# Filter scores of a batch taken in one place, by row halves into two PSUM banks

## The chip, the cores and the metric

The kernel runs on one core of a Trainium2 chip. The metric is the device time of one execution in microseconds, as the median of several runs; less is better. A core has a matrix engine (TensorE: PE in the rows, its weight loads PEld), a vector engine (VectorE: DVE), an activation engine (ScalarE: ACT), a general engine (GpSimd: POOL) and a queue for transfers (SyncE: SP). Matrix results land in PSUM, here eight banks of 512 floats for each of 128 partitions; the other engines take them from there.

## The reference, cut to what matters

A layer normalisation, an attention and a mixture of experts with product keys, all added to the input. The case has 16 batches of 256 tokens and a width of 128. The change lies in the mixture, in the step that is called the filter here: the scores `s0`, `s1` and their best four.

```python
x = L0_attn_x                                   # [16, 256, 128]
xn = layernorm(x)
x = x + attention(xn) + experts(xn)             # attention: 16 heads of 8
# experts
q = (xn @ Wq + bq).reshape(B, S, 8, 32)         # 8 heads of 32 features
q = batchnorm(q)
q0, q1 = l2norm(q[..., :16]), l2norm(q[..., 16:])
s0 = einsum('bshq,kq->bshk', q0, l2norm(sub_key0))    # 32 scores for each head and side
s1 = einsum('bshq,kq->bshk', q1, l2norm(sub_key1))
ts0, ti0 = top_k(s0, 4); ts1, ti1 = top_k(s1, 4)
w = softmax(all 16 sums of a pair); idx = 32 * ti0 + ti1
out = sum over pairs of up[idx] * gelu(down[idx] . xn) * w
```

## The kernel before

The program has one instruction stream for each engine, written by hand, and the engines meet by counting semaphores. After the inputs are projected (up to about 56 us) comes one long loop of 128 slots, eight to each of the 16 batches, one for each pair of attention heads. I call the slot's number modulo eight k. Every stream walks the same slots, and what it does in a slot, and in what order, is fixed by the code.

In every slot PE takes the second scores of one pair (`sj`, L651: K times Q into the PSUM tensor `SJ`), the first scores of a later pair (`si`, L615, into `SI`), and in every second slot the attention's values (`values`, L675: sixteen matmul instructions into the bank `psO`). DVE reduces each `si` to its maxima (L1002), ACT takes the exponential of each `sj` (L449). `SJ` has one copy, so `sj` of the next slot waits for the exponential of this one. `psO` holds two halves, one for each eight heads: `values` fills a half in two slots (k=2 and 4, or k=6 and the next 0), and ACT copies it out a slot later (L419, into `Osb`, semaphore `o_ev`; in k=1 the half that k=0 completed).

Between these lie the filter's steps of an earlier batch. Nearly all of their PSUM results go through one bank, `psM`, one after the other:

- k=0: POOL has split the row maxima (L1276, L1278, semaphore `ms`), PE transposes them into `psM` (`turn_maxima`, L695), ACT copies them out (L463), and two small DMAs on SP carry them to where `sj` of k=3 reads them (`max_rows`, L283).
- k=1: PE takes the scores of the batch's first 128 tokens into `psM` (`scores`, L705; the lines L709 are its matmuls): two matmuls, each of 128 feature rows by 256 columns, the keys `kblk` being block diagonal. In float32 a matmul is two matmul instructions.
- k=2: ACT copies them to `s_sb` (L410), DVE takes the best eight of each group of 32 (L1028, 16 instructions). After `values` and `si` PE takes the scores of the second 128 tokens (L796 waits until ACT's copy has freed `psM`).
- k=3: ACT copies them, DVE takes their best eight; PE waits for that copy (L804) before it transposes the products of another batch into `psM` (`turn_products`, L713; L716).
- k=3 and 4: ACT takes the best four (`best_four`, L377). k=4 to 7: DVE marks them with sixteen match-and-replace steps (L1052), and POOL works out ranks and weights. In k=5 ACT copies a transposed output (L456), DVE inverts its denominators (L1060, `rden`), and POOL, which waits for that, normalises (L1218, `on`). After it come POOL's rank steps, and behind these in the same queue the split of the maxima for the next k=0.

The scores of batch 0 come while other work is under way, those of batch 15 after the loop, in two banks of `SI` (L815). The token tiles and heads of a batch are numbered 0 to 15 in `s_sb`: eight heads of the first tile, then eight of the second.

Of the kernel before, what the change touches and what calls it, by code (L numbers as in the profile page):

```python
# [24 lines left out]
ACT = mybir.ActivationFunctionType  # L25
AX = mybir.AxisListType.X

P = 128
# [18 lines left out]
def program(nc, x, Wq, bq, Wl, bl, Wk, bk, Wv, bv, Wo, bo,  # L47
            fWq, fbq, gamma, beta, key0, key1, down, up, const, scratch, out):
    B, S, D = x.shape
# [5 lines left out]
    BT = S // P  # L55
# [6 lines left out]
    FH, FQ = 8, 32  # L62
# [20 lines left out]
    with ctx:  # L83
# [85 lines left out]
        psG = [SJ[:, 0:512], SJ[:, 512:1024]]  # L169
        psS = [SI[0][:, 0:512], SI[0][:, 512:1024]]  # L170
# [3 lines left out]
        REPLACED = (0, 4, 10, 12, 16)  # L174

# [134 lines left out]
        def _(act):  # L310
# [66 lines left out]
            def best_four(b, t):  # L377
                hs = slice(FH * t, FH * (t + 1))
                act.wait_ge(s["t8"], 2 * b + t + 1)
                if b >= 1:  # L380
                    act.wait_ge(s["mr"], 4 * b)
                A(top4[:, hs, 0:TOP], top8[:, hs, 1, 0:TOP], ACT.Copy).then_inc(s["t4"], 1)

            for slot in range(NSLOT):
# [17 lines left out]
                if k in (2, 3) and 0 <= b < B:  # L402

                    t = k - 2
                    act.wait_ge(s["fs"], 2 * b + t + 1)
                    act.wait_ge(s["pad"], 1)
                    if b >= 1:
                        act.wait_ge(s["mr"], 4 * b)
                        act.wait_ge(s["sel"], b)
                    A(s_sb[:, FH * t:FH * (t + 1), :, 0:NK].rearrange("p h a k -> p (h a) k"),  # L410
                      psM.rearrange("p (g k) -> p g k", k=NK), ACT.Copy).then_inc(s["fs_ev"], 1)
# [68 lines left out]
            def last_scores(t):  # L480
                act.wait_ge(s["fs"], 2 * LB + t + 1)
                A(s_last[:, FH * t:FH * (t + 1), :, 0:NK].rearrange("p h a k -> p (h a) k"),
                  psS[t].rearrange("p (g k) -> p g k", k=NK), ACT.Copy).then_inc(s["fs_ev"], 1)
# [47 lines left out]
        def _(pe):  # L531
# [173 lines left out]
            def scores(b, t, dst):  # L705

                tok = (BT * b + t) * P
                for r in range(2):
                    last = mm(dst[:, 256 * r:256 * (r + 1)], fqT[:, r, tok:tok + P],  # L709
                              kblk[:, :, :].rearrange("p g k -> p (g k)"), start=True, stop=True)  # L710
                last.then_inc(s["fs"], 1)
# [39 lines left out]
            for slot in range(NSLOT):  # L751
# [14 lines left out]
                if m >= 0 and m % 2 == 0:  # L766
                    values(m // 2)
                if slot < NPAIR * B - 1:

                    si(slot + 1)  # L770
                if FILTER <= slot < FILTER + NC:
                    norms(slot - FILTER)
# [15 lines left out]
                if k in (1, 2) and 0 <= b < B:  # L788

                    if b == 0 and k == 1:  # L790
                        pe.wait_ge(s["kblk"], 1)
                    if k == 1:
                        pe.wait_ge(s["mt_ev"], b + 1)
                        pe.wait_ge(s["ff"], b + 1)
                    else:
                        pe.wait_ge(s["fs_ev"], 2 * b + 1)  # L796
                    scores(b, k - 1, psM)
# [17 lines left out]
            for t in range(BT):  # L815
                scores(LB, t, psS[t])
# [47 lines left out]
        def _(dve):  # L864
# [128 lines left out]
            for slot in range(NSLOT):  # L993
# [25 lines left out]
                if k in (2, 3) and 0 <= b < B:  # L1019

                    t = k - 2
                    dve.wait_ge(s["fs_ev"], 2 * b + t + 1)
                    if b >= 1:
                        dve.wait_ge(s["sel"], b)
                        dve.wait_ge(s["t4"], 2 * b)
                    for h in range(FH * t, FH * (t + 1)):
                        for a in range(2):
                            last = V.max(top8[:, h, a, :], s_sb[:, h, a, 0:NK])  # L1028
                    last.then_inc(s["t8"], 1)
# [10 lines left out]
                if k in (4, 5, 6, 7) and 0 <= b < B:  # L1040

                    quarter = k - 4
                    t = quarter // 2
                    dve.wait_ge(s["t4"], 2 * b + t + 1)
                    if b >= 1:
                        dve.wait_ge(s["pr"], 4 * b - 2 * (1 - t))
                    for h in range(REPLACED[quarter], REPLACED[quarter + 1]):
                        if quarter == 1 and h == FH:
                            dve.wait_ge(s["t4"], 2 * b + 2)
                            if b >= 1:  # L1050
                                dve.wait_ge(s["pr"], 4 * b)
                        last = V.match_replace(r_sb[:, h, :], top4[:, h, :], s_sb[:, h, 1, :], NEG)  # L1052
                    last.then_inc(s["mr"], 1)
# [38 lines left out]
            for t in range(2):  # L1092
                dve.wait_ge(s["fs_ev"], 2 * LB + t + 1)
                for h in range(FH * t, FH * (t + 1)):
                    for a in range(2):
                        last = V.max(top8[:, h, a, :], s_last[:, h, a, 0:NK])
                last.then_inc(s["t8"], 1)
            for t in range(2):
                dve.wait_ge(s["t4"], 2 * LB + t + 1)
# [53 lines left out]
        def _(pool):  # L1153
# [166 lines left out]
            for t in range(2):  # L1320
# [11 lines left out]
                pool.wait_ge(s["t8"], 2 * b + t + 1)  # L1332
                pool.wait_ge(s["mr"], 4 * b)
                V.tensor_copy(top4[:, hs, 0:TOP], top8[:, hs, 1, 0:TOP]).then_inc(s["t4"], 1)
# [60 lines left out]
```

## Time and profile before

| | |
|---|---|
| median of 3 runs | 353.02 us (352.87 to 353.14) |
| the profiled execution | 350.41 us |
| its span, first to last instruction | 348.3 us |
| busy: PE, DVE, ACT, POOL | 311.8, 320.7, 265.2, 274.0 us |
| mean granted TensorE clock | 0.99 of full speed |
| largest groups | DVE L1002 153.2 us, ACT L449 119.2 us, PE L690 68.7 us |

The page of the profile has a chain of work that ended last, which it follows back from the last instruction: 63% of it is PE, 17% ACT and 9% DVE. All rows are from that one execution. In the rows of the timeline a line gives the start from the beginning of the span, the time from the first start to the last end of the instructions merged in it, engine and line, the operation, the tensors out<-in, the shapes out<-in, how many (x), and in brackets how long the engine stood idle before it and what ended that. An instruction on DVE or ACT can start a little before the one ahead of it has ended, so two neighbours can overlap by some hundredths.

### The profile page before, as it was taken

What the parts mean: (1) busy time and instruction counts of PE and PEld (TensorE: products, weight loads), DVE (VectorE), ACT (ScalarE), POOL (GpSimd) and SP (SyncE); (2) the same over time, 40 slices, a digit from 0 to 9 for tenths busy, and PEclk for the clock granted to TensorE, in tenths of its full rate; (3) what the DMA queues carried; (4) which work ended last, traced back from release to release, by engine and by line L of the source; (5) the groups of instructions that cost most, each with busy time, mean ns of one, the idle gap of its engine ahead of it and who ended that gap; (6) DMA issues with size and microseconds to landing.
All of it is one profiled execution on the core that took longest, in us unless ns stands there. A gap on an engine that the chain in (4) does not pass through costs nothing.

```text
span 348.3 us, 9625 instructions
## 1 busy us (share of the span) xinstructions
PE 311.8 (90%) x3024; PEld 168.1 (48%) x3024; DVE 320.7 (92%) x1393; ACT 265.2 (76%) x446; POOL 274.0 (79%) x527
## 2 busy tenths in 40 slices
PE   3898997976999999999999989999999999998886
PEld 2455554332445554545454545454544545555445
DVE  6599989989999999999999999999999999999681
ACT  3699995978687877787768686868677787878781
POOL 6288885835869898989898989888898989898930
PEclk9999999996999999999999999999999999999999
DMA  4765666217121112213030303030303030000001
GB/s 122 212 172 138 175 179 179 75 53 128 37 63 48 47 51 60 78 34 93 18 91 22 108 3 109 2 108 5 108 19 92 19 92 20 3 20 1 19 17 30
DMA packets 45886, 24.81 MB, mean 71 GB/s; under 512 B 5452, under 2 KB 45708, under 8 KB 45836
## 3 DMA queue, kind: packets, MB, share of 16 engines
q1 hardware_dynamic: 45836, 24.20, 25.9%
q8 instruction: 24, 0.39, 0.5%
q14 instruction: 26, 0.21, 0.2%
HBM read 15.54 MB, written 8.39 MB: 69 GB/s over the span
## 4 chain that ended last, share of the span: by engine, by line
PE 63%; ACT 17%; DVE 9%; issue 8%; POOL 1%; ACTq 0%; POOLq 0%; DVEq 0%
PE bank L690 13%; PE SJ L670 9%; PE bank L716 9%; PE bank L709 9%; PE SI L629 6%; ACT Eb L449 5%; PE bank L744 3%; ACT s_sb L410 3%; PE SJ L779 2%; ACT onT L432 2%; PE bank L745 2%; ACT fwq_in L456 2%; PE bank L736 2%; PE bank L646 1%; ACT fqT L328 1%
## 5 line engine op out<-in xcount | busy, mean ns | idle before, releaser
L1002 DVE TENSOR_REDUCE negm<-SI 128x4 f32<-128x1024 f32 x128 | 153.2, 1208 | 1.0 <-PE SI L629 1.0
L449 ACT ACTIVATE Eb<-SJ 128x1024 f32<-128x1024 f32 x117 | 119.2, 1019 | 10.3 <-PE SJ L670 10.2
L690 PE MATMUL bank<-Eb,vhat 128*18 128x256 f32 x1024 | 68.7, 386 | 0.9 <-ACT Osb L488 0.9
L670 PE MATMUL SJ<-QS,KS 50*128 50x256 bf16 x484 | 48.2, 278 | 10.3 <-ACT Eb L449 9.8
L1305 POOL TENSOR_TENSOR prod<-r_sb,a 128x1024 f32<-128x1024 f32 x28 | 53.5, 1910 | 0.0
L629 PE MATMUL SI<-KS,QS 48*128 48x256 bf16 x512 | 50.6, 277 | 1.8 <-DVE negm L1002 1.8
L1028 DVE MAX8 top<-s_sb 128x8 f32<-128x32 f32 x480 | 47.6, 177 | 2.9 <-ACT s_sb L410 0.8
L1052 DVE MATCH_REPLACE8 r_sb<-top,s_sb 128x36 f32<-128x36 f32 x240 | 40.5, 181 | 0.0
L690 PEld LDWEIGHTS bank<-Eb,vhat 128*18 128x18 f32 x1024 | 24.2, 98 | 26.8 <-issue 13.7
L629 PEld LDWEIGHTS SI<-KS,QS 48*128 48x128 bf16 x512 | 18.7, 95 | 35.2 <-issue 21.1
L716 PE MATMUL bank<-cst,prod 128*128 128x128 f32 x240 | 32.4, 278 | 3.3 <-ACT s_sb L410 3.3
L709 PE MATMUL bank<-kblk,fqT 128*128 128x256 f32 x120 | 33.9, 405 | 0.4 <-ACT s_sb L410 0.4
L410 ACT ACTIVATE s_sb<-bank 128x512 f32<-128x512 f32 x30 | 17.9, 596 | 20.2 <-PE bank L709 19.3
L670 PEld LDWEIGHTS SJ<-QS,KS 50*128 50x128 bf16 x484 | 14.0, 95 | 38.8 <-ACT Eb L449 27.1
L716 PEld LDWEIGHTS bank<-cst,prod 128*128 128x128 f32 x240 | 25.7, 141 | 10.4 <-issue 9.9
L1175 POOL TENSOR_TENSOR Eb<-Eb,parts 128x512 f32<-128x512 f32 x16 | 18.2, 1156 | 15.7 <-ACT parts L318 11.8
L709 PEld LDWEIGHTS bank<-kblk,fqT 128*128 128x128 f32 x120 | 20.3, 189 | 8.3 <-issue 3.1
L1052 DVE MATCH_VALUE_LOAD r_sb<-top,s_sb 128x8 f32 x240 | 19.1, 80 | 0.0
L1218 POOL TENSOR_TENSOR on<-fwq_in,rden 128x256 f32<-128x256 f32 x14 | 8.8, 630 | 10.5 <-DVE rden L1060 10.5
L1241 POOL TENSOR_TENSOR z_sb<-s_sb,rn 128x64 f32<-128x64 f32 x15 | 4.6, 306 | 15.3 <-DVE top L1028 15.3
L744 PE MATMUL bank<-wo_sb,onT 128*128 128x128 f32 x60 | 13.0, 299 | 3.7 <-ACT onT L432 3.7
L1267 POOL TENSOR_TENSOR rank<-rank,ties 128x48 f32<-128x48 f32 (+2 forms) x45 | 12.4, 275 | 4.5
(213 smaller groups left out, 622.5 us busy)
## 6 DMA issues: line engine op xcount, KB each, us to landing
qk_parts<-parts SPq DMA_DIRECT2D x48, 128.0 KB, 2.4
QS<-qk_parts SPq DMA_DIRECT2D x32, 96.0 KB
KS<-qk_parts SPq DMA_DIRECT2D x32, 96.0 KB
x_sb<-L_attn_x SPq DMA_DIRECT2D x8, 256.0 KB, 3.4
QS<-qk_parts SPq DMA_DIRECT2D x32, 64.0 KB
KS<-qk_parts SPq DMA_DIRECT2D x32, 64.0 KB
out<-ysb SPq DMA_DIRECT2D x16, 128.0 KB, 2.3
QS<-qk_parts SPq DMA_DIRECT2D x32, 32.0 KB
```

What stands on the lines that cost most here:

```text
L410: A(s_sb[:, FH * t:FH * (t + 1), :, 0:NK].rearrange("p h a k -> p (h a) k"), psM.rearrange("p (g k) -> p g k", k=NK), ACT.Copy).then_inc(s ...
L449: A(Eb[:, n % 4, :], SJ[:, :], ACT.Exp).then_inc(s["ex"], 1)
L629: last = mm(SI[n % 2][:, (e * BT + t) * S:(e * BT + t + 1) * S], QS[r, b % RING, pr, t * P:(t + 1) * P], KS[r, b % RING, pr, :], start=Tru ...
L670: last = mm(second(n)[:, (e * BT + t) * S:(e * BT + t + 1) * S], KS[r, b % RING, pr, t * P:(t + 1) * P], QS[r, b % RING, pr, :], start=Tru ...
L690: last = mm(psO[32 * c:32 * c + 2 * VC, (q % 2) * S:(q % 2 + 1) * S], vhat[:, v0:v0 + 2 * VC], Eb[:, (2 * g + c // 2) % 4, e0:e0 + S], sta ...
L709: last = mm(dst[:, 256 * r:256 * (r + 1)], fqT[:, r, tok:tok + P], kblk[:, :, :].rearrange("p g k -> p (g k)"), start=True, stop=True)
L716: last = mm(dst[:, t * P:(t + 1) * P], prod[:, t, h, :, :].rearrange("p i j -> p (i j)"), ident, start=(h == 0), stop=(h == FH - 1), is_tr ...
L744: mm(psM[:, t * D:(t + 1) * D], onT[:, t * P:(t + 1) * P], wo_sb[:, :], start=True, stop=False)
L1002: V.tensor_reduce(negm[:, bb % 2, :, :, pr].rearrange("p t e -> p e t"), SI[slot % 2][:, :].rearrange("p (e t j) -> p e t j", e=2, j=S), a ...
L1028: last = V.max(top8[:, h, a, :], s_sb[:, h, a, 0:NK])
L1052: last = V.match_replace(r_sb[:, h, :], top4[:, h, :], s_sb[:, h, 1, :], NEG)
L1305: TT(prod[:, t, :, :, :], r_sb[:, hs, 0:NK].unsqueeze(2).to_broadcast([P, FH, TOP, NK]), a0[:, hs, :].unsqueeze(3).to_broadcast([P, FH, TO ...
```

## The change

Of batches 1 to 14 the scores of both token tiles are now taken in k=1, ahead of `sj` of k=2. They are not split by tokens but by feature rows: rows 0 to 63 (four groups of 32 scores for each tile and r) go to `psM`, rows 64 to 127 to `psO`, so that a matmul has 64 rows and 128 columns, and there are eight in place of four, alternating between the two halves. Before them PE waits for the copy of the finished half of `psO` (`o_ev`). In k=2 ACT makes both copies, one after the other, ahead of its exponential; `values` of k=2 moves behind `si` and waits for both copies. The order in which DVE visits the heads follows the halves (`HEADS`), and so do the copies of the best four. Batch 0 keeps its two places but is split by halves as well; batch 15 takes all at once into the two banks of `SI`.

```diff
+        psH = [psM, psO]
+        HEADS = [4 * q + 2 * e + u for e in range(2) for q in range(NH // 4) for u in range(2)]
+        def half(a, e):
+            if len(a.shape) == 3:
+                return a.rearrange("p (q e u) k -> p q e u k", e=2, u=2)[:, :, e, :, :]
+            return a.rearrange("p (q e u) a k -> p q e u a k", e=2, u=2)[:, :, e, :, :, :]
@@ ACT @@
+            def filter_scores(to, e, src):
+                A(half(to[:, :, :, 0:NK], e).rearrange("p q u a k -> p q (u a) k"),
+                  src.rearrange("p (q g k) -> p q g k", g=4, k=NK), ACT.Copy).then_inc(s["fs_ev"], 1)
-                if k in (2, 3) and 0 <= b < B:
-                    t = k - 2
-                    act.wait_ge(s["fs"], 2 * b + t + 1)
...
+                if k == 2 and 1 <= b < B:
+                    act.wait_ge(s["fs"], 2 * b + 2)
+                    act.wait_ge(s["mr"], 4 * b)
+                    act.wait_ge(s["sel"], b)
+                    for e in range(2):
+                        filter_scores(s_sb, e, psH[e])
@@ PE @@
-            def scores(b, t, dst):
-                tok = (BT * b + t) * P
-                for r in range(2):
-                    last = mm(dst[:, 256 * r:256 * (r + 1)], fqT[:, r, tok:tok + P],
-                              kblk[:, :, :].rearrange("p g k -> p (g k)"), start=True, stop=True)
-                last.then_inc(s["fs"], 1)
+            def scores(b, halves, dst):
+                for q in range(2 * BT):
+                    t, r = q // 2, q % 2
+                    tok = (BT * b + t) * P
+                    for e in halves:
+                        rows = slice(64 * e, 64 * (e + 1))
+                        last = mm(dst[e][:, q * P:(q + 1) * P], fqT[rows, r, tok:tok + P],
+                                  kblk[rows, 4 * e:4 * (e + 1), :].rearrange("p g k -> p (g k)"), start=True, stop=True)
+                last.then_inc(s["fs"], len(halves))
-                if m >= 0 and m % 2 == 0:
+                if m >= 0 and m % 2 == 0 and k != 2:
                     values(m // 2)
                 if slot < NPAIR * B - 1:
                     si(slot + 1)
+                if m >= 0 and k == 2:
+                    pe.wait_ge(s["fs_ev"], 2 * (slot // 8))
+                    values(m // 2)
...
+                if k == 1 and 1 <= b < B:
+                    pe.wait_ge(s["mt_ev"], b + 1)
+                    pe.wait_ge(s["ff"], b + 1)
+                    pe.wait_ge(s["o_ev"], 2 * b - 1)
+                    scores(b, (0, 1), psH)
...
-            for t in range(BT):
-                scores(LB, t, psS[t])
+            scores(LB, (0, 1), psS)
@@ DVE @@
-                        dve.wait_ge(s["pr"], 4 * b - 2 * (1 - t))
+                        dve.wait_ge(s["pr"], 4 * b)
...
@@ POOL, last batch @@
-                pool.wait_ge(s["t8"], 2 * b + t + 1)
-                pool.wait_ge(s["mr"], 4 * b)
-                V.tensor_copy(top4[:, hs, 0:TOP], top8[:, hs, 1, 0:TOP]).then_inc(s["t4"], 1)
+                if t == 0:
+                    pool.wait_ge(s["mr"], 4 * b)
+                    for e in range(2):
+                        pool.wait_ge(s["t8"], 2 * b + e + 1)
+                        V.tensor_copy(half(top4[:, :, 0:TOP], e), half(top8[:, :, 1, 0:TOP], e)).then_inc(s["t4"], 1)
```

## Rows read from the trace of the kernel before

**Rows 1.** Busy time by stretch: length; PE, PEld, DVE, ACT, POOL busy; granted clock; DMA.
```profile
56.00:73.00 17.00, 15.24 (x172) 6.25 (x168) 15.76 (x22) 15.54 (x21) 14.23 (x10) 1.00 0.34 92
73.00:89.60 16.60, 10.46 (x98) 4.86 (x99) 15.71 (x80) 12.71 (x17) 6.47 (x18) 0.79 0.50 96
...
222.33:238.91 16.58, 15.62 (x170) 8.32 (x170) 16.30 (x77) 12.78 (x21) 14.57 (x32) 1.00 0.21 58
```

**Rows 2.** Chain of waits in one batch: start, length, engine and line.
```profile
221.85 0.22 PE bank L744 x2
...
228.60 0.61 ACT s_sb L410
...
229.34 1.06 PE bank L716 x8
...
236.36 0.05 issue
```

**Rows 3.** Timeline of PE, k=0 to k=3 of the same batch.
```profile
223.87 0.29 PE L701 MATMUL bank<-cst,mpart 128*32 128x128 bf16 x2
224.09 0.39 PE L670 MATMUL SJ<-QS,KS 50*128 50x256 bf16 x4
224.32 0.39 PE L629 MATMUL SI<-KS,QS 48*128 48x256 bf16 x4
224.63 1.13 PE L709 MATMUL bank<-kblk,fqT 128*128 128x256 f32 x4
225.79 0.39 PE L670 MATMUL SJ<-QS,KS 50*128 50x256 bf16 x4
226.12 1.06 PE L690 MATMUL bank<-Eb,vhat 128*18 128x256 f32 x16
...
227.43 1.13 PE L709 MATMUL bank<-kblk,fqT 128*128 128x256 f32 x4
228.49 0.39 PE L670 MATMUL SJ<-QS,KS 50*128 50x256 bf16 x4
```

**Rows 4.** Timeline of ACT, the same batch.
```profile
224.19 0.37 ACT L463 ACTIVATE mT<-bank 32x256 bf16<-32x256 f32 x1 [0.50 <-PE bank L701]
224.47 0.36 ACT L419 ACTIVATE Osb<-bank 128x256 f32<-128x256 f32 x1
...
225.80 0.60 ACT L410 ACTIVATE s_sb<-bank 128x512 f32<-128x512 f32 x1
226.29 1.02 ACT L449 ACTIVATE Eb<-SJ 128x1024 f32<-128x1024 f32 x1
...
234.35 0.41 ACT L456 ACTIVATE fwq_in<-bank 128x288 f32<-128x288 f32 x1
```

**Rows 5.** Timeline of DVE, the same batch.
```profile
223.98 2.36 DVE L1002 TENSOR_REDUCE negm<-SI 128x4 f32<-128x1024 f32 x2
226.43 1.59 DVE L1028 MAX8 top<-s_sb 128x8 f32<-128x32 f32 x16
227.94 1.21 DVE L1002 TENSOR_REDUCE negm<-SI 128x4 f32<-128x1024 f32 x1
229.23 1.59 DVE L1028 MAX8 top<-s_sb 128x8 f32<-128x32 f32 x16
...
234.54 0.18 DVE L1052 MATCH_REPLACE8 r_sb<-top,s_sb 128x36 f32<-128x36 f32 x1
234.79 0.35 DVE L1060 RECIPROCAL rden<-fwq_in 128x32 f32<-128x32 f32 x1
```

**Rows 6.** Timeline of POOL, the same batch.
```profile
223.21 0.25 POOL L1278 TENSOR_TENSOR mpart<-negm,mpart 128x32 bf16<-128x32 f32 x1
...
235.22 0.63 POOL L1218 TENSOR_TENSOR on<-fwq_in,rden 128x256 f32<-128x256 f32 x1 [0.75 <-DVE rden L1060]
```

**Rows 7.** Timeline of PE behind the loop: the scores of batch 15.
```profile
321.65 1.89 PE L709 MATMUL SI<-kblk,fqT 128*128 128x256 f32 x8
```

**Rows 8.** Timeline of POOL behind the loop: a copy of the best four.
```profile
327.19 0.21 POOL L1334 COPY top<-top 128x32 f32<-128x32 f32 x1
```

More of the change, by code:

```diff
@@ L375, in _, with best_four @@
             first_part(NC - 1, 1)
-            def best_four(b, t):
-                hs = slice(FH * t, FH * (t + 1))
-                act.wait_ge(s["t8"], 2 * b + t + 1)
+            def filter_scores(to, e, src):
+                A(half(to[:, :, :, 0:NK], e).rearrange("p q u a k -> p q (u a) k"),
+                  src.rearrange("p (q g k) -> p q g k", g=4, k=NK), ACT.Copy).then_inc(s["fs_ev"], 1)
+            def best_four(b, e):
+                act.wait_ge(s["t8"], 2 * b + e + 1)
                 if b >= 1:
                     act.wait_ge(s["mr"], 4 * b)
-                A(top4[:, hs, 0:TOP], top8[:, hs, 1, 0:TOP], ACT.Copy).then_inc(s["t4"], 1)
+                A(half(top4[:, :, 0:TOP], e), half(top8[:, :, 1, 0:TOP], e), ACT.Copy).then_inc(s["t4"], 1)
             for slot in range(NSLOT):
@@ L401, in _ @@
                 b = slot // 8 - 1
-                if k in (2, 3) and 0 <= b < B:
-                    t = k - 2
-                    act.wait_ge(s["fs"], 2 * b + t + 1)
+                if b == 0 and k in (2, 3):
+                    act.wait_ge(s["fs"], k - 1)
                     act.wait_ge(s["pad"], 1)
[L407 to L411, printed above, removed]
+                    filter_scores(s_sb, k - 2, psM)
+                if k == 2 and 1 <= b < B:
[4 more added lines that the diff above has]
+                        filter_scores(s_sb, e, psH[e])
                 m = slot - LAG - 6
@@ L478, in weights, with last_scores @@
                 A(Eb[:, n % 4, :], second(n)[:, :], ACT.Exp).then_inc(s["ex"], 1)
[L480 to L483, printed above, removed]
+            def last_scores(e):
+                act.wait_ge(s["fs"], 2 * LB + 2)
+                filter_scores(s_last, e, psS[e])
             def outputs(q):
@@ L787, in _ @@
                     turn_maxima(b)
-                if k in (1, 2) and 0 <= b < B:
-                    if b == 0 and k == 1:
+                if b == 0 and k in (1, 2):
+                    if k == 1:
                         pe.wait_ge(s["kblk"], 1)
-                    if k == 1:
-                        pe.wait_ge(s["mt_ev"], b + 1)
-                        pe.wait_ge(s["ff"], b + 1)
-                    else:
-                        pe.wait_ge(s["fs_ev"], 2 * b + 1)
-                    scores(b, k - 1, psM)
+                        pe.wait_ge(s["mt_ev"], 1)
+                        pe.wait_ge(s["ff"], 1)
+                    else:
+                        pe.wait_ge(s["fs_ev"], 1)
+                    scores(0, (k - 1,), [psM, psM])
+                if k == 1 and 1 <= b < B:
[3 more added lines that the diff above has]
+                    scores(b, (0, 1), psH)
                 b = (slot - LAG - 8) // 8
@@ L1025, in _ @@
                         dve.wait_ge(s["t4"], 2 * b)
-                    for h in range(FH * t, FH * (t + 1)):
+                    for h in HEADS[FH * t:FH * (t + 1)]:
                         for a in range(2):
@@ L1045, in _ @@
                     if b >= 1:
-                        dve.wait_ge(s["pr"], 4 * b - 2 * (1 - t))
-                    for h in range(REPLACED[quarter], REPLACED[quarter + 1]):
-                        if quarter == 1 and h == FH:
+                        dve.wait_ge(s["pr"], 4 * b)
+                    for i in range(REPLACED[quarter], REPLACED[quarter + 1]):
+                        if quarter == 1 and i == FH:
                             dve.wait_ge(s["t4"], 2 * b + 2)
-                            if b >= 1:
-                                dve.wait_ge(s["pr"], 4 * b)
+                        h = HEADS[i]
                         last = V.match_replace(r_sb[:, h, :], top4[:, h, :], s_sb[:, h, 1, :], NEG)
@@ L1093, in _ @@
                 dve.wait_ge(s["fs_ev"], 2 * LB + t + 1)
-                for h in range(FH * t, FH * (t + 1)):
+                for h in HEADS[FH * t:FH * (t + 1)]:
                     for a in range(2):
@@ L1098, in _ @@
             for t in range(2):
-                dve.wait_ge(s["t4"], 2 * LB + t + 1)
+                dve.wait_ge(s["t4"], 2 * LB + 2)
                 dve.wait_ge(s["pr"], 4 * LB - 2 * (1 - t))
```

## The prediction

> **What bounds the kernel now.** I read three views in this order: busy time by stretch, the chain of waits over one batch, and the timelines of the four engines over the same batch. The stretch shows a loop that repeats every 16.58 us, with PE busy for 15.62 and DVE for 16.30 of it at a granted clock of 1.00, that is 2.4 GHz [rows 1]. So two engines are nearly full, and shortening one alone need not shorten the loop. The chain of waits runs over PE almost without a break from k=0 to k=5, except at one place: in k=3 PE has finished `sj`, and `turn_products` can only start at 229.34, because ACT's copy of the second scores ran from 228.60 for 0.61 [rows 2]. The timelines show the slack beside the chain. Three figures matter:
>
> - DVE stands three times a batch. Its next instruction usually starts 0.08 before the one ahead has ended (226.43 + 1.59 = 228.02, but the reduction starts at 227.94) [rows 5]. Ahead of the first MAX8 it stands 226.43 - 226.34 + 0.08 = 0.17, ahead of the second 229.23 - 229.15 + 0.08 = 0.16, and ahead of `rden` 234.79 - 234.72 + 0.08 = 0.15 [rows 5]. The first two end with a score copy (225.80 + 0.60 = 226.40; the second at 229.20), the third with ACT's copy at 234.76 [rows 2, 4]. Together 0.48: no rearrangement of the scores can take more than that from a batch, as DVE has the same instructions afterwards.
> - POOL's split of the maxima ends at 223.21 + 0.25 = 223.46, and PE transposes it only at 223.87 [rows 3, 6]. A wake takes 0.05 (the chain's "issue" before `sj`) [rows 2], so there PE could come 0.36 earlier.
> - POOL's `on` waits 0.75 for `rden` [rows 6], and behind `on` stand POOL's rank steps and the next split. So DVE's time decides when PE gets its maxima.
>
> **The change, part by part.** I take PE's `turn_maxima` (223.87) as zero point of a batch and follow it through.
>
> *Start of the scores.* Now PE starts them at 224.63, 0.07 behind ACT's L463 (224.56) [rows 3, 4]. The new wait is for `o_ev`, the copy L419, which ends at 224.83 [rows 4]. Behind the waiting instruction stand `sj`, `si` and `values` of k=2. Start at 224.90: +0.27.
>
> *Length of the block.* Removed are two blocks of 1.13 (four instructions of 256 columns each), added is one of sixteen instructions of 64 rows and 128 columns. An instruction of 128 columns in float32 costs 0.11 (two in 0.22) [rows 2], so four of 256 cost 0.88, and a block has 0.25 beside that. What the trace does not show is whether two float32 matmuls of 64 rows run side by side. If they do: 8 x 0.11 + 0.25 = 1.13, as long as one old block. If they don't: 16 x 0.11 + 0.25 = 2.01. Two rows are near. `sj` and `si` are split into the same two row halves, in bfloat16: four matmuls of 256 columns give way after 0.23 (224.09 to 224.32) [rows 3], and at one column in a tick of 2.4 GHz four in turn would take 0.43. And `values` is float32 in four column groups: its sixteen instructions of 256 columns span 1.06 [rows 3], and in turn they would take 16 x 0.22 = 3.5. Splitting works for the halves and works for float32, so I take 1.13. The scores then end 0.27 later than the first scores do now, at 224.63 + 1.13 + 0.27 = 226.03.
>
> The Trainium skill speaks against this in "TensorE: Matmul & The Clock Gate", section "LDWEIGHTS": the load of weights costs by columns, and one of 32 rows takes as long as one of 128. By it the halves double the loads from 8 to 16 a batch, and if these queued, the second length would hold (the first rival below). No run here shows float32 loads of two row halves.
>
> *Copies and MAX8.* The first copy starts 0.04 after the scores and ends at 226.67 (now 226.40); the second follows 0.49 later (the present distance from L410 to the next start) [rows 4] and ends at 227.16. The first MAX8 is later by 0.27, but the second no longer waits: the reduction between them ends after 227.16. DVE leaves the scores 0.27 - 0.16 = 0.11 later.
>
> *PE in k=2 and k=3.* `sj` and `si` run at once; then PE stands for the second copy until about 227.16 + 0.1. This wait of some 0.9 is new; behind it are `values`, `sj` of k=3 and all PE work, and ACT waits with it for that `sj`. `values` takes 0.99 (226.12 to the next block), so `sj` of k=3 starts at 228.25 instead of 228.49 [rows 3]. ACT's exponential of k=2 moves from 226.29 to 227.04 [rows 4] and ends at 228.06, just ahead of it. `turn_products` then starts after `sj` and `si`, 0.55 later, at 228.80 instead of 229.34 [rows 2]: PE and ACT are 0.54 earlier through k=4 to k=7, the copy that ended DVE's wait for `rden` among them.
>
> *Back at the start.* `rden`: 0.11 - 0.15 = 0.04 earlier in the first such batch, and with it `on` and POOL's split; PE, 0.54 early, meets the split 0.04 + 0.36 = 0.40 early. From then on the loop is bound by the circle from split over `turn_maxima`, scores, first copy, MAX8, DVE, `rden`, `on` back to the split. Its change per batch is 0.27 - 0.16 - 0.15 - 0.36 = -0.40, which I round to -0.39 for the hundredths in the rows. This is less than DVE's 0.48 and PE's 0.54, so it binds.
>
> *At nothing.* The order of heads, the best four by halves, and the later wait for `pr` of both tiles change no count; POOL's products are long done by k=4. The DMAs that carry the maxima leave when L463 ends, as before. Batch 0 keeps two blocks of eight instructions of 128 columns, one after another: 8 x 0.11 + 0.25 = 1.13, as now. Behind the loop the scores of batch 15 get shorter than their 1.89 [rows 7], but `turn_maxima` behind them waits for POOL's split, which the circle already counts; POOL makes a 0.21 copy [rows 8] ahead of the second product rather than behind it, and DVE's steps there waited for both anyway. Without that cover it would cost 0.2.
>
> *Sum.* Batches 1 to 14: 14 x -0.39 = -5.5. The profiled execution would take 350.41 - 5.5 = 344.9 with a span of 342.8. The median of the runs lies 2.6 above the profiled one; I carry that over: 353.02 - 5.5 = 347.5.
>
> **Rivals.**
>
> 1. *The halves queue in PE.* Place: the sixteen matmuls. Block 2.01, scores later by 0.27 + 0.88 = 1.15; the circle changes by 1.15 - 0.67 = +0.48, 14 x 0.48 = +6.7: 359.7, slower. It decides from a block of 1.13 + 0.40 = 1.53 on. For it: no float32 row halves in the trace. Against it: the two rows above. Chance 0.10.
> 2. *The halves overlap only in part.* With one instruction's 0.11 left over in the block the circle gains 0.29, 349.0 (chance 0.12, same sign). At a block of about 1.5 nothing is left, 353.0: the change then doesn't do what it says. Chance 0.04.
> 3. *DVE is the bound.* If PE starts sooner than I think, DVE's 0.48 is the end: 14 x 0.48 = 6.7, 346.3. For it: DVE's 16.30 of 16.58 [rows 1]. Chance 0.14.
> 4. *The clock falls in the new gap of 0.9.* In the stretch with PE busy for 10.46 of 16.60 the granted clock was 0.79; in the one ahead of it, with 15.24 of 17.00, it was 1.00 [rows 1]. The new batch has 15.62 - 1.13 = 14.5 of 16.2, much nearer to the second. Priced by the first row, 14.5 / 0.79 - 14.5 = 3.9 a batch, over 50 us; chance 0.02.
>
> **How the numbers follow.** My forecast has 0.58. The range takes in it and the cases of the same sign (346.3 to 349.0) with the unknown hundredths of the wakes, 14 x 0.03 = 0.4 below and, above, another 0.11 in the block (14 x 0.07 = 1.0): 345.9 to 350.0. Faster by over 0.2% (0.7 us, about what a measurement of this kernel can tell from no change): 0.58 + 0.12 + 0.14 = 0.84; within: 0.04; slower: 0.12.
>
> **What would show it.** In the trace after: one block of scores per batch from batch 1 on, about 1.1 long, starting 0.07 after L419; its length decides between forecast and first rival. The two copies 0.49 apart; no wait of DVE ahead of the second MAX8 and of `rden`; PE standing some 0.9 ahead of `values` in k=2, and waiting for POOL ahead of `turn_maxima`, as it does not before the change; a batch of 16.2. I am wrong if PE's wait in k=2 is much above 1, if ACT's exponential of k=2 comes after `values`, or if the clock is below 1.00 in the loop.

## The result and the profile after

| | before | after |
|---|---|---|
| median of the runs | 352.94 us (352.36 to 353.14) | 348.03 us (346.52 to 349.47) |
| the profiled execution | 350.41 | 346.52 |
| its span | 348.3 | 344.5 |
| from `turn_maxima` of batch 1 to that of batch 15 | 232.92 | 228.76 |

The time after is 0.9876 of the time before (95% interval 0.9840 to 0.9912; the two medians divided give 0.986). Some executions of one experiment below, in_turn, were slow at a lower granted clock, and its median and ratio leave them out. The forecast was 347.5. Within the loop the forecast was 5.5 less and the profiles show 4.16 less; why the time came nearer to the forecast than the loop is taken up below.

The page of the kernel after, its first two lines and the engines' share of the chain of waits:

```profile
span 344.5 us, 9824 instructions
...
PE 296.4 (86%) x3152; PEld 165.9 (48%) x3152; DVE 317.3 (92%) x1393; ACT 265.7 (77%) x446; POOL 274.4 (80%) x527
...
DVE 32%; PE 32%; ACT 13%; POOL 13%; issue 9%; POOLq 0%; ACTq 0%; DVEq 0%
```

PE is busy for 15.4 us less, and it held 63% of the chain before; now DVE and PE hold a third each and POOL, which was not among the first three, holds as much as ACT. The chain of waits over one batch shows the loop that the prediction called the circle (start, length, engine and line):

```profile
221.72 0.26 POOL mpart L1297
...
222.02 0.30 PE bank L712 x2
...
222.63 0.37 ACT Osb L431
223.00 0.14 issue
223.13 1.18 PE bank L723 x16
...
224.33 0.61 ACT s_sb L386
...
224.96 0.65 DVE top L1048 x6
...
233.07 0.27 DVE rden L1079
...
233.41 0.63 POOL on L1237
...
238.28 0.30 PE bank L712 x2
```

In order: split, `turn_maxima`, the copy of the attention output's half (new in it), scores, first copy, DVE's long row of work, `rden`, `on`, POOL's rank steps, the next split. A batch is 238.28 - 222.02 = 16.26, against 16.58 [rows 1]. The timeline of PE over the same batch has the block that decided between the forecast and its first rival:

```profile
222.02 0.29 PE L712 MATMUL bank<-cst,mpart 128*32 128x128 bf16 x2
222.24 0.39 PE L681 MATMUL SJ<-QS,KS 50*128 50x256 bf16 x4
222.47 0.38 PE L640 MATMUL SI<-KS,QS 48*128 48x256 bf16 x4
223.13 1.16 PE L723 MATMUL bank<-kblk,fqT 64*128 64x128 f32 x16 [0.27 <-ACT Osb L431]
...
225.47 1.06 PE L701 MATMUL bank<-Eb,vhat 128*18 128x256 f32 x16 [0.73 <-ACT s_sb L386]
```

Sixteen instructions of 64 rows span 1.16, so the two row halves run side by side, and one block does the work of the two blocks of 1.13 [rows 3]. PE starts it late, for the `Osb` copy, and stands 0.73 ahead of `values`, for the score copies. DVE's timeline answers rows 5:

```profile
224.96 1.59 DVE L1048 MAX8 top<-s_sb 128x8 f32<-128x32 f32 x16 [0.18 <-ACT s_sb L386]
226.46 1.22 DVE L1022 TENSOR_REDUCE negm<-SI 128x4 f32<-128x1024 f32 x1
227.58 1.58 DVE L1048 MAX8 top<-s_sb 128x8 f32<-128x32 f32 x16
...
232.97 0.36 DVE L1079 RECIPROCAL rden<-fwq_in 128x32 f32<-128x32 f32 x1
```

The second MAX8 starts 0.10 before the reduction ahead of it has ended (226.46 + 1.22 = 227.68), and `rden` follows the last replacement as closely: two of DVE's three waits are gone. The first is left.

One batch is different. From the `turn_maxima` at 188.84 to the one at 205.76 it is 16.91 (16.914 before the starts are rounded), and POOL's timeline there shows why:

```profile
204.50 0.20 POOL L1336 MEMSET fqT<- 128x128 f32 x1
204.65 0.21 POOL L1295 CAST mpart<-negm 128x32 bf16<-128x32 f32 x1
204.95 0.75 POOL L1297 TENSOR_TENSOR mpart<-negm,mpart 128x32 bf16<-128x32 f32 x1
205.67 0.32 POOL L1302 TENSOR_TENSOR p<-rank,z_sb 128x64 f32<-128x64 f32 x1
```

Once in the program, in slot 68, POOL fills the padding of `s_last` (L1336) ahead of the split. The split's second step takes 0.75 there and 0.24 or 0.25 in every other batch; the step behind it, `p`, takes 0.32 there and 0.77 in an ordinary batch.

### The profile page after: what moved, and what is told of

It is laid out like the page before. It is cut to its first block, busy times and chain, and to the rows that moved or that the text cites. A ratio compares the mean times of both kernels' runs of the same rounds, so it can differ in the third digit from the quotient of the medians.

```text
span 344.5 us, 9824 instructions
## 1 busy us (share of the span) xinstructions
PE 296.4 (86%) x3152; PEld 165.9 (48%) x3152; DVE 317.3 (92%) x1393; ACT 265.7 (77%) x446; POOL 274.4 (80%) x527
## 4 chain that ended last, share of the span: by engine, by line
DVE 32%; PE 32%; ACT 13%; POOL 13%; issue 9%; POOLq 0%; ACTq 0%; DVEq 0%
DVE negm L1022 9%; DVE top L1048 9%; PE bank L701 6%; PE bank L723 5%; DVE r_sb L1071 5%; PE bank L730 3%; PE SJ L681 3%; ACT s_sb L386 3%; ACT Eb L461 3%; POOL rank L1286 2%; POOL cmp L1276 2%; PE SI L640 2%; PE SJ L796 2%; POOL on L1237 2%; ACT Osb L431 1%
## 5 line engine op out<-in xcount | busy, mean ns | idle before, releaser
L681 PE MATMUL SJ<-QS,KS 50*128 50x256 bf16 x484 | 48.9, 279 | 9.0 <-ACT Eb L461 9.0
L640 PE MATMUL SI<-KS,QS 48*128 48x256 bf16 x512 | 51.6, 277 | 1.8 <-DVE negm L1022 1.8
L640 PEld LDWEIGHTS SI<-KS,QS 48*128 48x128 bf16 x512 | 21.2, 96 | 28.8 <-issue 20.7
L681 PEld LDWEIGHTS SJ<-QS,KS 50*128 50x128 bf16 x484 | 16.2, 95 | 33.3 <-ACT Eb L461 20.5
L723 PE MATMUL bank<-kblk,fqT 64*128 64x128 f32 x240 | 18.6, 283 | 4.3 <-ACT Osb L431 3.8
L386 ACT ACTIVATE s_sb<-bank 128x512 f32<-128x512 f32 x30 | 16.4, 594 | 7.4 <-PE bank L723 7.4
L1071 DVE MATCH_VALUE_LOAD r_sb<-top,s_sb 128x8 f32 x240 | 20.1, 84 | 0.0
L723 PEld LDWEIGHTS bank<-kblk,fqT 64*128 64x128 f32 x240 | 15.9, 187 | 8.3 <-ACT mT L475 7.4
L1263 POOL TENSOR_TENSOR z_sb<-s_sb,rn 128x512 f32<-128x512 f32 x15 | 15.9, 1061 | 0.0
```

Source lines behind the costliest of these rows:

```text
L386: A(half(to[:, :, :, 0:NK], e).rearrange("p q u a k -> p q (u a) k"), src.rearrange("p (q g k) -> p q g k", g=4, k=NK), ACT.Copy).then_inc ...
L640: last = mm(SI[n % 2][:, (e * BT + t) * S:(e * BT + t + 1) * S], QS[r, b % RING, pr, t * P:(t + 1) * P], KS[r, b % RING, pr, :], start=Tru ...
L681: last = mm(second(n)[:, (e * BT + t) * S:(e * BT + t + 1) * S], KS[r, b % RING, pr, t * P:(t + 1) * P], QS[r, b % RING, pr, :], start=Tru ...
L723: last = mm(dst[e][:, q * P:(q + 1) * P], fqT[rows, r, tok:tok + P], kblk[rows, 4 * e:4 * (e + 1), :].rearrange("p g k -> p (g k)"), start ...
```

## The experiments

Batches were compared from one `turn_maxima` to the next, as the circle runs through it. Times ahead of batch 1 differ from one execution to the next of the same kernel (see **before_again**), so times of whole runs scatter by some 3 us, while an ordinary batch repeats within some hundredths. A ratio compares a kernel with the kernel before that was timed beside it.

| kernel | median us | of before (95%) | batch us |
|---|---|---|---|
| before | 352.9 (352.6 beside whole_rows, both_first, before_both; 353.3 beside memset_gap) | | 16.58 |
| the change, again | 347.99 | 0.9871 (0.9832 to 0.9911) | 16.25 |
| in_turn | 353.64 | 1.0069 (1.0031 to 1.0107) | 16.77 |
| whole_rows | 358.38 | 1.0185 (1.0140 to 1.0230) | 17.06 |
| copy_first | 345.12 | 0.9798 (0.9756 to 0.9840) | 15.98 |
| split_first | 345.78 | 0.9819 (0.9780 to 0.9857) | 16.14 |
| both_first | 343.58 | 0.9762 (0.9726 to 0.9799) | 15.99 |
| before_both | 351.61 | 0.9971 (0.9937 to 1.0005) | 16.49 |
| memset_gap | 347.06 (one run) | | 16.26 |

**after_again**: no edit; the change beside the first experiments, for their common scale.

> The changed kernel unaltered, once more, as the base of the runs beside it. Its four runs so far lie in two groups, 346.5 to 347.0 and 349.1 to 349.5, which is wider than the whole spread of the kernel before (352.4 to 353.1). Theory A (the spread belongs to the kernel: its stretch at the lower granted clock from about 78 to 95 us falls differently from run to run): the times spread over 2 to 3 us again, a batch lasts 16.26 us in every profile, and the median is 348 with a ratio near 0.987. Theory B (two of the four were chance): all runs lie within 1 us of each other.

347.99 and a batch of 16.25. It repeats, and the batch with POOL's fill is again 16.91. The six runs lie between 346.43 and 349.08, so the spread belongs to the kernel, as theory A has it.

**in_turn**: the same sixteen instructions, but one row half after the other.

```diff
-                for q in range(2 * BT):
-                    t, r = q // 2, q % 2
-                    tok = (BT * b + t) * P
-                    for e in halves:
+                for e in halves:
+                    for q in range(2 * BT):
+                        t, r = q // 2, q % 2
+                        tok = (BT * b + t) * P
                         rows = slice(64 * e, 64 * (e + 1))
```

> The changed kernel, with the sixteen score instructions of a batch in another order: first the eight of the upper rows, then the eight of the lower rows, in place of alternating. Number, shape and banks are the same. Theory 1 (float32 matmuls of two row halves run side by side only when they alternate, and the block lies on the circle): the block grows from 1.16 to 1.9 to 2.0 us, a batch from 16.26 to about 17.1, 14 x 0.8 = 11 us more than the changed kernel, about 359, slower than the kernel before by 1.8%. Rival (the engine pairs them whatever the order, or never did): block and time as in the changed kernel.

The profile has three batches at a granted clock of 0.91, of 18.21, 18.22 and 18.44 us (this one the last of the loop); what the order costs is read from the others, at 1.00 (stretches of the two kinds: length; PE, PEld, DVE, ACT, POOL busy; granted clock; DMA):

```profile
179.28:196.05 16.77, 15.02 (x177) 8.61 (x177) 16.06 (x77) 12.79 (x21) 14.59 (x32) 1.00 0.21 58
230.25:248.47 18.22, 16.51 (x176) 9.16 (x177) 16.61 (x77) 12.79 (x21) 15.00 (x32) 0.91 0.20 53
```

A batch of 16.77, 0.51 longer than with the halves alternating, and slower than before the change. The block in the timeline of PE:

```profile
180.38 1.35 PE L723 MATMUL bank<-kblk,fqT 64*128 64x128 f32 x13 [0.27 <-ACT Osb L431]
181.47 0.28 PE L681 MATMUL SJ<-QS,KS 50*128 50x256 bf16 x1
181.57 0.27 PE L723 MATMUL bank<-kblk,fqT 64*128 64x128 f32 x1
181.59 0.27 PE L681 MATMUL SJ<-QS,KS 50*128 50x256 bf16 x1
181.68 0.27 PE L723 MATMUL bank<-kblk,fqT 64*128 64x128 f32 x1
181.70 0.27 PE L640 MATMUL SI<-KS,QS 48*128 48x256 bf16 x1
181.79 0.27 PE L723 MATMUL bank<-kblk,fqT 64*128 64x128 f32 x1
```

It runs from 180.38 to 181.79 + 0.27 = 182.06: 1.68, where 2.01 was the price of halves that queue. So the expectation of 17.1 was a miss. The last three score instructions start among instructions of `sj` and `si`, which stand behind them in the program but use the row half that is already free. The first thirteen span 1.35, where thirteen in a queue would span 13 x 0.11 + 0.25 = 1.68. So even in this order part of the work lay side by side, where the second half sets in before the first is through, and the rest was filled by what follows. That the alternation is worth 0.52 of block and 0.51 of batch is shown.

**whole_rows**: the kernel before with both scores in one place, ordered as in the change, but split by tokens, so that each instruction has all 128 rows and 256 columns. The heads keep their old order. Its matmuls, against the kernel before:

```diff
-            def scores(b, t, dst):
-                tok = (BT * b + t) * P
-                for r in range(2):
-                    last = mm(dst[:, 256 * r:256 * (r + 1)], fqT[:, r, tok:tok + P],
-                              kblk[:, :, :].rearrange("p g k -> p (g k)"), start=True, stop=True)
-                last.then_inc(s["fs"], 1)
+            def scores(b, halves, dst):
+                for t in halves:
+                    tok = (BT * b + t) * P
+                    for r in range(2):
+                        last = mm(dst[t][:, 256 * r:256 * (r + 1)], fqT[:, r, tok:tok + P],
+                                  kblk[:, :, :].rearrange("p g k -> p (g k)"), start=True, stop=True)
+                last.then_inc(s["fs"], len(halves))
```

> The changed kernel without the row halves: the scores of both token tiles are still taken at once in k=1, but by tokens, one tile to each of the two banks, in four matmuls of 128 rows and 256 columns. Theory 1 (the block lies on the circle, one for one): the block is twice 0.88 and 0.25 us, 2.0 in place of 1.16, a batch 16.26 + 0.84 = 17.1 us, 14 x 0.84 = 11.8 us more than the changed kernel, about 359.8, slower than the kernel before. Rival (the gain is that both tiles are taken in one place, and PE has time to spare there): a batch at or below the 16.58 us of the kernel before.

PE's timeline from one `turn_maxima` to the next, with the block between, and then DVE's first MAX8:

```profile
228.13 0.29 PE L710 MATMUL bank<-cst,mpart 128*32 128x128 bf16 x2
...
229.24 1.97 PE L719 MATMUL bank<-kblk,fqT 128*128 128x256 f32 x8 [0.27 <-ACT Osb L429]
...
245.19 0.29 PE L710 MATMUL bank<-cst,mpart 128*32 128x128 bf16 x2
```

```profile
231.87 1.58 DVE L1044 MAX8 top<-s_sb 128x8 f32<-128x32 f32 x16 [0.98 <-ACT s_sb L384]
```

The block is 1.97 and the batch 245.19 - 228.13 = 17.06, as expected. Against the change that is 0.81 more in the block and 0.80 more in the batch; DVE stands 0.98 ahead of its first MAX8 instead of 0.18, the same 0.80. Against the kernel before, timed beside it at 352.56, taking the scores in one place loses 5.8 us by itself: the whole gain is in the row halves. With in_turn it also shows that the block lies on what binds, one for one. Which circle that is these two runs can't tell, since the second circle, found in split_first, holds the block as well. By this slope the change would break even at a block of 1.16 + (16.58 - 16.26) = 1.48; the prediction put that point at 1.53.

**copy_first**: the copy of the finished `psO` half is moved ahead of L475 in ACT's order, to where ACT stands anyway for `turn_maxima`.

```diff
+                def output_copy(m):
                     q = m // 4
                     act.wait_ge(s["pv"], 2 * q + 2)
...
+                m = slot - LAG - 6
+                if m >= 0 and m % 4 == 0 and m // 4 < 2 * B and k != 1:
+                    output_copy(m)
...
+                if k == 0 and slot + 1 - LAG - 6 >= 0:
+                    output_copy(slot + 1 - LAG - 6)
                 if k == 0 and 0 <= b < B:
```

> The changed kernel, with one thing moved on ACT: the copy of the finished half of psO, which ACT makes in k=1 behind the copy of the turned maxima, is made in k=0 ahead of it, while ACT stands waiting for the transpose. Theory 1 (a batch is bound by the circle from POOL's split over the transpose, the copy of psO, the scores, their first copy, MAX8 and DVE to rden and back to POOL): the scores start 0.33 earlier after the transpose, and a batch falls from 16.26 to 16.0 us, where DVE's remaining 0.25 us of waiting ahead of the first MAX8 is used up; 14 batches give 3.5 us less than the changed kernel, ratio to the kernel before about 0.977. Theory 2 (DVE alone bounds the batch): a batch stays at 16.26 us and the time the same. Theory 3 (PE's wait for both score copies bounds it): 0.33 us a batch, 4.6 us less.

ACT now makes the copy at 220.59, ahead of `turn_maxima`. In PE's timeline the scores no longer wait for it:

```profile
220.88 0.29 PE L716 MATMUL bank<-cst,mpart 128*32 128x128 bf16 x2
...
221.63 1.16 PE L727 MATMUL bank<-kblk,fqT 64*128 64x128 f32 x16
...
236.86 0.29 PE L716 MATMUL bank<-cst,mpart 128*32 128x128 bf16 x2
```

The scores start 0.75 behind `turn_maxima`, as before the change [rows 3], instead of 1.11. Of these 0.36 the batch gains 0.28 (15.98) and DVE's wait ahead of the first MAX8 is gone: now DVE has none left.

**split_first**: POOL's split of the maxima is moved up, between its rank steps.

```diff
+            def split(bm):
+                pool.wait_ge(s["mx"], NPAIR * (bm + 1))
+                if bm >= 1:
+                    pool.wait_ge(s["mt"], bm)
+                most = negm[:, bm % 2, :, :, :]
+                V.tensor_copy(mpart[:, :, :, 0, :], most).then_inc(s["mh"], 1)
+                pool.wait_ge(s["mh"], bm + 1)
+                TT(mpart[:, :, :, 1, :], most, mpart[:, :, :, 0, :], ALU.subtract).then_inc(s["ms"], 1)
...
+                        if i == 0 and b + 1 < B:
+                            split(b + 1)
...
-                bm = slot // 8
-                if k == 7 and bm < B:
...
+                if slot == 7:
+                    split(0)
```

> The changed kernel, with one thing moved on POOL: the split of the row maxima is made after the first of the three rank additions, as soon as DVE's last reduction of the batch is there, in place of after all rank steps. That ends it about 1.1 us earlier. Theory 1 (the circle through POOL's split): the circle has more than enough to spare, and the batch falls to the next bound, DVE at 16.0 us; 14 batches give 3.5 us less than the changed kernel, ratio to the kernel before about 0.977. Theory 2 (DVE alone bounds) and theory 3 (PE's wait for both score copies bounds): 16.26 us a batch as before, the same time.

The split now ends 1.17 ahead of `turn_maxima`, and the batch is 16.14. That is a gain of 0.12: the circle through POOL did bind, as theory 1 has it, but the next bound is not DVE, which would have given 0.26 (16.0). The chain of waits in that batch no longer touches DVE or POOL:

```profile
221.18 0.37 ACT Osb L431
...
221.68 1.18 PE bank L723 x16
...
223.37 0.60 ACT s_sb L386
...
224.02 1.06 PE bank L701 x16
...
231.58 1.04 ACT Eb L461
...
235.47 0.99 PE bank L701 x16
```

So with the split out of the way a second circle binds: `turn_maxima`, `Osb` copy, scores, both copies, `values`, and PE and ACT in turn to the end of the batch. In the change it lay only 16.26 - 16.14 = 0.12 behind the first. All batches but the last (15.82) are 16.14, the one with POOL's fill too: the fill (204.34) now stands behind the split (203.02) in POOL's order and no longer delays it.

**both_first**: copy_first and split_first together.

> The changed kernel with both moves at once: ACT copies the finished half of psO in k=0 ahead of the turned maxima, and POOL splits the maxima after the first rank addition. Alone they took a batch from 16.26 to 15.98 us (the copy) and to 16.14 us (the split). Theory 1 (the circle through POOL is gone, DVE is next, whose instructions without any wait come to about 15.9 us a batch): 15.9 to 16.0 us, at most 1.4 us less than with the copy alone, the time 343.5 to 345.0. Theory 2 (the moves act on different waits and add up): 16.26 - 0.28 - 0.12 = 15.86 us, 343.4.

343.58, the shortest of all, 0.9762 of before. Two batches in a row:

```profile
205.27:221.25 15.98, 14.73 (x178) 7.96 (x176) 15.95 (x77) 13.08 (x22) 14.64 (x33) 1.00 0.23 61
221.26:237.25 15.99, 14.73 (x179) 7.94 (x177) 15.96 (x77) 13.09 (x22) 14.58 (x32) 1.00 0.23 60
```

DVE is busy for 15.95 of 15.98 and the split ends 0.82 ahead of its need: DVE alone is the bound. In the first three batches `turn_maxima` comes after 15.90, 15.79 and 15.84, but DVE's own round, from the second on, is 15.98 (L1089 at 109.61 and at 125.59): PE gets ahead of DVE once, by 0.4 in all. After that the moves add nothing to each other in an ordinary batch (copy_first has the same 15.98); split_first's share is this lead, the fill, which costs nothing here, and the last batch (15.66 against 16.45).

**before_both**: the same two moves in the kernel before.

> The kernel before with the same two moves and nothing else of the change. Theory 1 (before the change PE's chain from k=0 to k=5 bounds a batch, POOL's split has 0.36 us to spare and nothing on PE waits for the copy of psO in k=1): a batch stays at 16.58 us, the time at that of the kernel before within 0.2%. Rival (the moves are good by themselves, and the circle has nothing to do with the change): 0.3 us a batch, about 4 us less.

A batch of 16.49, 0.09 less than before, where 16.58 was expected; 351.61, a ratio whose interval reaches to 1.0005. The miss has a reason in ACT's timeline:

```profile
225.39 0.37 ACT L467 ACTIVATE mT<-bank 32x256 bf16<-32x256 f32 x1
225.72 1.02 ACT L451 ACTIVATE Eb<-SJ 128x1024 f32<-128x1024 f32 x1
```

The exponential of k=1 follows L467 at once, since the `Osb` copy is no longer between them, and `sj` of k=2 needs it. That `sj` starts 1.83 behind `turn_maxima` (226.89 - 225.06) instead of 1.92 (225.79 - 223.87) [rows 3], and the batch gains these 0.09. From batch 1 to 15 the two moves are worth 232.92 - 231.45 = 1.5 in the kernel before, and 228.76 - 223.09 = 5.7 in the changed one: they pay where the circle over POOL and the `Osb` copy binds, and there the change put it.

**memset_gap**: POOL's fill moves from slot 68 to a place ahead of `on`, where POOL stands for `rden`.

```diff
                     if b >= 1:
                         gated(b - 1)
+                        if slot == 67:
+                            pool.wait_ge(s["fs"], 10)
+                            V.memset(s_last[:, :, :, NK:KP], NEG).then_inc(s["pad2"], 1)
                         normalised(b - 1)
...
-                if slot == 68:
-
-                    pool.wait_ge(s["fs"], 10)
-                    V.memset(s_last[:, :, :, NK:KP], NEG).then_inc(s["pad2"], 1)
```

> The changed kernel with one instruction moved: POOL's single fill of the padding for batch 15, which it makes in slot 68 between its rank steps and the split of the maxima, is made in slot 67 ahead of its wait for rden, where it stands 0.6 us. Theory A (with POOL on the circle, the fill puts the split of that one batch under DVE's masking step, L1085, and the split then takes 0.75 in place of 0.25 us): the one batch of 16.91 us becomes 16.26 like the others, and the kernel is 0.65 us shorter between the second and the last transpose of the maxima. Rival (the long batch comes from something else there): it stays at 16.91 us. The whole time differs by less than the runs of one kernel do among each other, and is not the measure.

The same batch in the timeline of PE:

```profile
190.02 0.29 PE L712 MATMUL bank<-cst,mpart 128*32 128x128 bf16 x2
...
206.29 0.29 PE L712 MATMUL bank<-cst,mpart 128*32 128x128 bf16 x2
```

16.27 in place of 16.91: the fill of 0.20 cost 0.65.

**before_again**: no edit; the kernel before, profiled again, for the scatter of the whole runs.

> The kernel before unaltered, for a second profile. Its times lie in two groups, 350.5 to 350.7 and 352.1 to 353.4; the profile that the prediction used is from the lower one. Theory A (the groups differ only ahead of batch 1, by where the stretch at the lower granted clock falls): the batches last 16.58 us again, and if the profile falls into the upper group, the transpose of the maxima of batch 1 comes 2 to 3 us later than at 90.88. Theory B (the groups differ in the loop): another length of batch.

This execution took 352.76, 2.35 more than the profile of before. Its ordinary batches are the same 16.58, but for the first, which is 16.77. The rest of the difference stands ahead of them: the `turn_maxima` of batch 1 starts at 93.12 instead of 90.88. From 76 to 96 us the granted clock was 0.74 here and 0.83 there; with the change it was 0.74 in one profile (90.88 became 91.28) and 0.57 in the other (93.94). So the mean clock alone doesn't give the shift: 0.74 goes with 93.12 in one kernel and with 91.28 in the other. The length of this early stretch differs between executions of either kernel, and what sets it isn't settled.

## Why the prediction was right, point by point

The circle in segments, from rows 3 to 6 and the timelines after:

| segment | before | after | difference | forecast |
|---|---|---|---|---|
| `turn_maxima` to scores | 0.76 | 1.11 | +0.35 | +0.27 |
| scores to first copy | 1.17 | 1.20 | +0.03 | 0 |
| first copy to MAX8 | 0.63 | 0.63 | 0 | 0 |
| MAX8 to `rden` | 8.36 | 8.01 | -0.35 | -0.31 |
| `rden` to `on` | 0.43 | 0.44 | +0.01 | 0 |
| `on` to the end of the split | 4.82 | 4.82 | 0 | 0 |
| split to `turn_maxima` | 0.41 | 0.05 | -0.36 | -0.36 |
| sum | 16.58 | 16.26 | -0.32 | -0.40 |

- **The circle binds.** Right. PE follows the split by 0.05, which it did not before; an earlier split shortens the batch (split_first), and a fill ahead of the split lengthens it in full (memset_gap). But by a hair: PE's own circle lay 0.12 behind, as split_first showed, where the forecast had 0.54 - 0.39 = 0.15; PE's circle gained 16.58 - 16.14 = 0.44 and not 0.54.
- **The halves run side by side.** Right, and it carries the gain: 1.16 against 1.13 forecast. The row that decided it was `sj`'s and `si`'s overlap of row halves, in bfloat16, beside `values` in float32 column groups [rows 3]; float32 row halves do as these did. The prediction held the doubled number of weight loads against this. A load of 64 rows does take as long as one of 128, 0.19 on average in both kernels, but the loads of the two halves overlap as well: the sixteen of a block stand within 1.00 (223.10 to 224.10).
- **Start of the scores.** The mechanism is right (the copy L431, and PE behind it), the size off: +0.35, not +0.27. The wake behind the copy (from its end to the matmul's start) took 0.14 in the chain, not the 0.07 that I took from the wait for L463, and `turn_maxima` to the end of the copy 0.97 (222.02 to 222.63 + 0.36) instead of 0.96. This is the mis-sized term of an ordinary batch: 0.08, and 0.04 more from the block and `on`, against 0.04 won back on DVE's way. The 0.14 stood in the rows before: `turn_products` starts 229.34 - 229.20 = 0.14 behind the copy that it waits for [rows 2]. The trace also has what these places have in common: in both, the late semaphore is checked by a wait instruction of its own ahead of the first weight load, which takes 0.05 (L804 before at 229.23, L817 after at 223.02), in 14 batches of 14; where 0.07 was seen, the load itself waits. In copy_first that wait instruction is through early (L821, 221.01 to 221.06), the load waits for the copy L479, and the same block starts 0.05 behind it.
- **The two waits of DVE, and the new gap of PE.** Right: both waits gone, and PE stands 0.73 ahead of `values` where some 0.9 was forecast. But 0.48 was not all that DVE had to give, as the prediction said. With no wait left a batch takes 15.98 (copy_first, both_first), 0.60 less than 16.58. A fourth wait was overlooked (rows below): behind the masking step the next reduction started only 224.01 - 223.98 = 0.03 before that step had ended, in place of 0.08, so 0.05 was lost there; the other 0.07 is in hundredths along DVE's way. So the third rival's price of 6.7 should have been 14 x 0.60 = 8.4. The clock in the loop stayed at 1.00, so the fourth rival didn't come.

```profile
223.33 0.68 DVE L1066 SCALAR_TENSOR_TENSOR r_sb<-r_sb,z_sb 128x512 f32<-128x512 f32 x1
223.98 2.36 DVE L1002 TENSOR_REDUCE negm<-SI 128x4 f32<-128x1024 f32 x2
```

- **Fourteen times the same.** Wrong for two of them. The batch with POOL's fill got 0.03 longer, not 0.39 shorter. Before the change the same fill pushed the same split by much the same, 0.67, but the 0.36 of slack between split and `turn_maxima` took over half of it (that batch was 16.88). I spent this slack in the circle's sum and didn't ask what else it had been hiding. The last batch gained 0.29.
- **Sum.** Twelve ordinary batches (-3.9 together), +0.03 and -0.29 make -4.16 between `turn_maxima` of batch 1 and batch 15; the forecast had -5.5. Of the 1.3 between them 0.8 is in the twelve, 0.4 in the batch with the fill and 0.1 in the last. Behind it both kernels take 24.5 (348.3 - 323.8 and 344.5 - 320.0): the part behind the loop is unchanged, as forecast. That 348.03 still lies so near to 347.5 is in part luck. For the profiled execution the forecast was 344.9, and 346.52 was measured, 1.6 more. To this the forecast added 2.6, by which the median before lay above its profile; after the change it lies only 1.5 above. The medians differ by 4.9, 0.7 more than the loop. Over the larger set beside after_again (17 and 6 runs) the means are 352.07 and 347.86, 4.2 apart, as the loop has it; so the 0.7 most likely comes from how the early stretch fell in a few runs, though no profile of those runs shows it.

Why POOL's step trebles there: in an ordinary batch the split starts at 221.72, ahead of DVE's masking step L1085 (221.83 to 222.52), and takes 0.25; it is `p`, behind it, that meets the masking and takes 0.77. In the batch with the fill the split starts at 204.95, just behind L1085 (204.92 to 205.60), and takes 0.75 itself, while `p` takes 0.32. L1085 takes 0.68 or 0.69 either way.

```profile
204.92 0.68 DVE L1085 SCALAR_TENSOR_TENSOR r_sb<-r_sb,z_sb 128x512 f32<-128x512 f32 x1
...
221.83 0.69 DVE L1085 SCALAR_TENSOR_TENSOR r_sb<-r_sb,z_sb 128x512 f32<-128x512 f32 x1
```

The Trainium skill has a rule for this in "SBUF — State Buffer", section "Who interferes with whom": a VectorE instruction with two inputs in SBUF and a GpSimd instruction that reads SBUF exclude each other, and the one issued first goes through. The trace agrees for the GpSimd instruction that comes second: 0.75 against 0.25 for the split, by 0.03 us of start. It doesn't show the other way round: behind a split that started 0.11 ahead of it L1085 takes 0.69, as against 0.68. So the 0.20 of the fill cost 0.15 of delay and 0.50 of being second.

## What to carry to other kernels

When a change is worth the slack between two engines, list everything that this slack covers, in the odd batches too, since what it hid (here a fill done once, 0.65 us) comes out in full. Follow the loop as a circle with a length for each segment, and also work out the next circle: here it lay 0.12 behind, so speeding up a part that only the first has pays no more than that. Read a wake from a place that waits in the same way: here it was 0.07 where the load itself waits, and 0.14 behind a wait instruction of its own, and both stood in the rows. Splitting a block-diagonal float32 matmul by rows paid because the order alternates between the halves; the same instructions half after half lost all of it.

## What the runs showed of the hardware

- Float32 matmuls of two row halves run side by side: sixteen instructions of 64 rows and 128 columns take 1.16 alternating (after), 1.68 half after half (in_turn); the same work as eight of 128 rows and 256 columns takes 1.97 (whole_rows).
- In the order of half after half (in_turn) the rows of PE have instructions of `sj` (181.47) starting ahead of older score instructions of the other row half (181.57 to 181.79).
- A PE matmul started 0.05 to 0.07 behind the end of the ACT copy that it waits for where its weight load carries the wait (before: scores behind L463; copy_first: scores behind L479), and 0.14 or 0.15 where a wait instruction of its own, of 0.05, stands ahead of the load (before: `turn_products` behind L410; after: scores behind L431). No run moved one and the same wait from one form to the other.
- In the profile of in_turn the granted clock was 0.91 over three batches, with PE busy for 15.0 of 16.77 in the batches that stayed at 1.00; in whole_rows no batch was like that. What set it off isn't settled.
- A VectorE step with two inputs in SBUF (L1085, 0.68) and a GpSimd step that starts 0.03 behind it: the GpSimd step took 0.75 instead of 0.25, and the VectorE step no longer than otherwise.
